# One transformer layer on one Trainium2 core: attention and last stage in one block with shared tiles, the first output projection between the last scores, the results added onto bias rows in memory

## What is computed

```python
x = x + attn(layernorm(x))      # 16 heads of 32; q = n @ Wq.T + bq + ocr_bias, k, v alike
                                # scores / sqrt(32) + 0.1 on |i - j| <= 2, softmax over 2048 keys, attn @ v
                                # out @ Wo.T + bo
x = x + ffn(layernorm(x))       # n and the weight are rounded per block of 32 to a 6-bit float grid times
                                # the block's scale (largest |n| / 7.5); then n_q @ w_q.T + bias
```

## Time and profile before

| | |
|---|---|
| median of 3 runs | 4273.5 us |
| the profiled execution | 4276.86 us |
| span of that execution, first to last instruction | 4275.0 us |
| mean granted TensorE clock | 0.983 |
| busy: TensorE, weight loads, VectorE, ScalarE, GpSimd | 97%, 60%, 77%, 56%, 70% |
| DMA queue of software (GpSimd's), share of 16 engines | 47.1% |
| DMA queue of hardware (SP's), share of 16 engines | 26.1% |

### The profile page before, as it was taken

The page is one execution under the profiler, slowest core; times in us unless marked ns, Lnnn a source line. Parts: engine busy times, 40 slices in busy tenths (PEclk is TensorE's granted clock), DMA queues, the critical chain, the costliest instruction groups (busy, mean ns, idle before and its releaser), DMA issues. The chain is left out here.

```text
span 4275.0 us, 60956 instructions
## 1 busy us (share of the span) xinstructions
PE 4150.8 (97%) x21904; PEld 2568.5 (60%) x21904; DVE 3302.9 (77%) x5623; ACT 2406.3 (56%) x4652; POOL 2988.7 (70%) x1047
## 2 busy tenths in 40 slices
PE   7999989999999999999999999999999999959999
PEld 6888855555555555555555555555555555527777
DVE  6444449888888888888888888888888888727776
ACT  2222215666667666666766666666666666633222
POOL 2111115888888888888888888888888888846552
PEclk9999988999999999999999999999999999979999
DMA  7666665888878878787887878878888787675442
GB/s 257 205 208 207 206 180 106 165 182 168 182 164 173 183 168 187 156 186 162 188 172 170 176 167 187 169 172 169 183 167 188 158 176 166 138 177 179 160 160 73
DMA packets 274636, 741.24 MB, mean 173 GB/s; under 512 B 27585, under 2 KB 94145, under 8 KB 220098
## 3 DMA queue, kind: packets, MB, share of 16 engines
q0 software_dynamic: 55296, 402.68, 47.1%
q1 hardware_dynamic: 219074, 335.10, 26.1%
HBM read 195.04 MB, written 139.46 MB: 78 GB/s over the span
## 5 line engine op out<-in xcount | busy, mean ns | idle before, releaser
L725 DVE TENSOR_REDUCE part_max<-ps_m 128x1 f32<-128x512 f32 x4096 | 2512.1, 679 | 441.9 <-PE ps_m L624 441.8
L790 POOL TENSOR_TENSOR pair<-p_sb 128x2048 f32<-128x2048 f32 x512 | 2419.4, 4769 | 259.8 <-ACT p_sb L715 148.8
L715 ACT ACTIVATE p_sb<-ps_s 128x512 f32<-128x512 f32 x4096 | 2083.3, 616 | 748.7 <-PE ps_s L643 745.3
L643 PE MATMUL ps_s<-q_st,k_st 97*128 97x512 f32 x4096 | 1685.9, 412 | 3.8 <-ACT p_sb L715 1.9
L624 PE MATMUL ps_m<-k_st,q_st 96*128 96x512 f32 x4096 | 1641.7, 404 | 20.3 <-POOL k_st L779 20.1
L643 PEld LDWEIGHTS ps_s<-q_st,k_st 97*128 97x128 f32 x4096 | 772.1, 189 | 648.3 <-issue 422.5
L657 PE MATMUL ps_o<-p_sb,v_sb 128*32 128x512 f32 x8192 | 988.0, 599 | 15.0 <-DVE p_sb L752 6.9
L624 PEld LDWEIGHTS ps_m<-k_st,q_st 96*128 96x128 f32 x4096 | 786.7, 192 | 191.5 <-DVE part_max L725 37.8
L657 PEld LDWEIGHTS ps_o<-p_sb,v_sb 128*32 128x32 f32 x8192 | 224.3, 109 | 493.1 <-ACT p_sb L715 310.3
L795 POOL DMA_DIRECT2D pair<-pair x384 | 336.2, 876 | 218.0 <-POOL pair L790 180.0
L172 POOL TENSOR_TENSOR xb<-xin,bo_row 128x2048 f32<-128x2048 f32 x16 | 75.3, 4703 | 428.6 <-DMA xin<-in_x 417.6
(11 more groups left out here) (97 smaller groups left out, 2621.6 us busy)
## 6 DMA issues: line engine op xcount, KB each, us to landing
pair<-pair POOLq DMA_DIRECT2D x384, 1024.0 KB, 8.6
q_st<-q_hi_d SPq DMA_DIRECT2D x128, 256.0 KB, 6.9
k_st<-k_hi_d SPq DMA_DIRECT2D x128, 256.0 KB, 9.3
xin<-in_x SPq DMA_DIRECT2D x16, 1024.0 KB, 8.3
xb_d<-xb SPq DMA_DIRECT2D x16, 1024.0 KB, 5.2
q_hi_d<-s_hi SPq DMA_DIRECT2D x64, 256.0 KB, 2.0
q_lo_d<-s_lo SPq DMA_DIRECT2D x64, 256.0 KB, 2.3
k_hi_d<-s_hi SPq DMA_DIRECT2D x64, 256.0 KB, 2.3
```

The lines of the kernel that those rows point to most:

```text
L643: nc.tensor.matmul(ps_s[:, (HG * s + h) % RING_S, :], k_st[0:ROWS + 1, unit // QC % 2, kt // TT, h, kt % TT * P:(kt % TT + 1) * P], q_st[0 ...
L715: nc.scalar.activation(p_sb[:, s % SLOTS, h, :], ps_s[:, (HG * s + h) % RING_S, :], ACT.Exp, scale=SCALE).then_inc(p_ready, 1)
L725: nc.vector.tensor_reduce(part_max[:, unit % 2, col, n:n + 1], ps_m[:, max_place(unit, j) % RING_M, :], AX.X, ALU.max).then_inc(max_taken, 1)
L790: nc.gpsimd.tensor_tensor(pair[:, m % PAIR_RING], p_sb[:, s % SLOTS], p_sb[:, (s + 1) % SLOTS], ALU.add).then_inc(paired, 1)
```

## The change

`attend` and `finish` become one function with one block. What it does:

- The barrier between the two stages goes. The last stage's tiles are laid over attention's: weights and `t_hi`, `t_lo`, `o_hi`, `o_rec` in `k_st`, `o_lo` in `q_st`, x1, `y`, `xd` and one `o_raw` in slots of `p_sb`, results in two slots of `pair`. `PAIR_RING` is 5. x1 and `xb` are one tile now (the residual is added in place), in a ring of 3; `o_rec` has one buffer in place of two.
- Chunk 0's output projection stands between the scores of the last unit, three matmuls behind every second score in steps 5 to 12. Chunks 0 and 1 are scaled and split on VectorE and ScalarE in that unit.
- The bias matmul of `linear` goes. In its place SP writes bias rows to the output in each of the first 16 units of attention, and the store of a chunk is an accumulating DMA issued by GpSimd.
- In the last stage, ScalarE's order is `high(c)`, `o_highs(c + 2)`, `normalise(c + 1)`; SP's is `load_o(c + 2)`, `load_rec(c + 2)`, `load_xb(c + 3)`.
- The sums of the last unit are finished inside the last stage.

```diff
-    PAIR_RING = 6
+    PAIR_RING = 5
+    FIRST_OUT = 5
...
+        o_first = sb("o_first", [P, NHG, CH])
+        o_hi, o_lo, o_rec = (k_st[:, 0, 0], q_st[:, 1]), (q_st[:, 0], q_st[:, 2]), f32(k_st[:, 0, 1])
+        wo_hi, wo_lo, wd_hi, wd_lo = k_st[:, 0, 2], k_st[:, 0, 3], k_st[:, 1, 0], k_st[:, 1, 1]
+        t_hi, t_lo = k_st[:, 1, 2], k_st[:, 1, 3]
+        x1 = (p_sb[:, 4], p_sb[:, 5], p_sb[:, 0])
+        y, xd, y_q = p_sb[:, 1], p_sb[:, 2], v_sb[:, 0:TT, :].bitcast(FP8)
+        res = (pair[:, 3], pair[:, 4])
+
+        def o_raw(c):
+            return p_sb[:, 3] if c > 1 and c % 2 == 0 else o_first
...
+            def load_o(c):
+                at_least(sp, o_split, NHG * (1 if c == 1 else c - 1))
+                sp.dma_start(o_raw(c)[:], o_by_chunk[c]).then_inc(o_in[c % 2], 16)
+
+            def load_rec(c):
+                at_least(sp, o_scaled, NHG * c)
+                sp.wait_ge(rec_out, 16 * (NG - QC + c // QC + 1))
+                for g in range(NHG):
+                    sp.dma_start(o_rec[:, g, :],
+                                 rec_d[g * NCH + c].unsqueeze(1).to_broadcast([HG, HD, CH])).then_inc(rec_in, 16)
+
+            def load_xb(c):
+                at_least(sp, res_ready, TT * (c - 2))
+                sp.dma_start(x1[c % 3], xb_d[c]).then_inc(xb_in[c % 3], 16)
...
+                    if unit < NCH and kt == 13:
+                        sp.dma_start(out_ch[unit], ffn_b.unsqueeze(0).unsqueeze(0).to_broadcast([P, TT, D])).then_inc(bias_out, 16)
...
+                    if unit == NU - 1 and kt == KT - 1:
+                        sp.wait_ge(pv_done, ST - 4)
+                        sp.wait_ge(paired, NM - 2)
+                        load_xb(0)
+            load_xb(1)
+            sp.wait_ge(scored, HG * ST)
+            sp.dma_start(f32(wd_hi), wd_hi_d).then_inc(wd_in, 16)
+            sp.dma_start(f32(wd_lo), wd_lo_d).then_inc(wd_in, 16)
+            sp.wait_ge(pv_done, ST)
+            sp.wait_ge(paired, NM)
+            load_xb(2)
+            for c in range(NCH):
+                if c + 2 < NCH:
+                    load_o(c + 2)
+                    load_rec(c + 2)
+                if c + 3 < NCH:
+                    load_xb(c + 3)
+                if c == 1:
+                    store_sum(NU - 1)
+                    load_den(NG - 1)
+                if c == 3:
+                    store_rec(NG - 1)
...
+            def between_scores(kt, h):
+
+                t, k = (kt - FIRST_OUT) // 2, (kt - FIRST_OUT) % 2 * 2 + h // 2
+                if h % 2 == 0 or not 0 <= t < TT:
+                    return
+                if k == 0:
+                    pe.wait_ge(max_taken, turn_no(NU - 1) + 1)
+                    if t == sum_place(NU - 2) % RING_M:
+                        pe.wait_ge(sum_copied, NU - 1)
+                out_part(0, t, k)
...
+            for c in range(NCH):
+                high(c)
+                if c + 2 < NCH:
+                    o_highs(c + 2)
+                if c + 1 < NCH:
+                    normalise(c + 1)
...
+            def store(c):
+                pool.wait_ge(res_ready, TT * c + TT)
+                pool.dma_start(out_ch[c], res[c % 2], accum_op=ALU.add).then_inc(out_done[c % 2], 16)
...
-                    nc.tensor.matmul(ps_r[:, t, :], ones2[:], fb[:], start=True, stop=False)
```

More of the change, by code:

```diff
@@ L569, in _ @@
                     if unit > 0:
-                        if kt == 8:
+                        if kt == 8 and unit < NU:
                             store_sum(unit - 1)
@@ L665, in add_keys @@
                     for h in range(HG):
-                        last = nc.tensor.matmul(ps_m[h * HD:(h + 1) * HD, bank, :], ones[:],
+                        last = nc.tensor.matmul(sum_bank(unit)[h * HD:(h + 1) * HD, :], ones[:],
                                                 pair[:, (PAIRS * unit + n) % PAIR_RING, h, :],
@@ L676, in burst, with out_part @@
                     add_keys(s // KT - 1)
+            def out_part(c, t, k):
+                if t == 0:
+                    pe.wait_ge(o_split, NHG * c + k + 1)
+                toks = slice(t * P, (t + 1) * P)
+                terms = ((o_hi[c % 2][:, k, toks], wo_hi[:, k, :]), (o_lo[c % 2][:, k, toks], wo_hi[:, k, :]),
+                         (o_hi[c % 2][:, k, toks], wo_lo[:, k, :]))
+                for j, (lhs, rhs) in enumerate(terms):
+                    if c == 0 and t == 0 and k == 0 and j != 1:
+                        pe.wait_ge(wo_in[j // 2], 16)
+                    last = nc.tensor.matmul(ps_r[:, t, :], lhs, rhs, start=(k == 0 and j == 0),
+                                            stop=(k == NHG - 1 and j == 2))
+                if k == NHG - 1:
+                    last.then_inc(out_projected, 1)
@@ new lines, in scale_o, with o_low @@
+            def scale_o(c):
+                v.wait_ge(o_in[c], 16)
+                v.wait_ge(rec_in, 16 * NHG * (c + 1))
+                for g in range(NHG):
+                    nc.vector.tensor_tensor(o_raw(c)[:, g, :], o_raw(c)[:, g, :], o_rec[:, g, :],
+                                            ALU.mult).then_inc(o_scaled, 1)
+            def o_low(c):
+                for g in range(NHG):
+                    v.wait_ge(o_high, NHG * c + g + 1)
+                    nc.vector.tensor_tensor(o_lo[c][:, g, :], o_raw(c)[:, g, :], f32(o_hi[c][:, g, :]),
+                                            ALU.subtract).then_inc(o_split, 1)
@@ L1088 @@
+                if c > 2:
+                    store(c - 3)
+            for c in range(NCH - 3, NCH):
+                store(c)
 def kernel(L0_attn_x, L0_attn_ocr_context, L0_attn_Wq, L0_attn_bq, L0_attn_Wk, L0_attn_bk, L0_attn_Wv,
```

477 lines of the change are left out of this document (210 added, 267 removed).

## The result

| | before | after |
|---|---|---|
| median of 4 runs | 4274.93 us | 4426.3 us (4424.11 to 4430.55) |
| ratio, 95% interval | | 1.0354 (1.0339 to 1.037) |
| span of the profiled execution | 4275.0 us | 4423.6 us |
| mean granted TensorE clock | 0.983 | 0.963 |

The kernel got 3.5% slower: 151 us more, where the prediction had 86. The sign and the loop are as forecast, and the time is 18 us above the upper end of the range. One execution of the last experiment was slow (4392.93 us at a granted clock of 0.893, its other five 4239.84 to 4247.28); its median of 4244.77 us counts it and is 4243.87 without.

What follows compares the result with a forecast made beforehand. TensorE bounded the last stage before; after the change a 37 us loop through the loads would: 3834 + 13 x 37 = 4315, then 23 and 22.7 more, span 4361, median 4359 us. Range 4320 to 4408.

Steps and rivals of the forecast that it cites:

- the loop: Last stage, one chunk's results to the next's through loads, scaling and normalisation: 37 us a chunk, bounds 34.0 and 43.
- the last unit: Attention's final unit: added matmuls and two `o_highs` show as +8 us, bounds 4 and 15.
- R(0): Moment VectorE finishes the last tile of chunk 0's results: 3834, 59 us earlier than before, 8 us either side.
- The 2 tenths: DMA engines' busy share while 1 MB of reciprocals loads: four of 16 engines, about 100 GB/s, 10.2 us.
- attention unchanged up to the last unit: Listed as a sign to see in the trace after: attention before its final unit keeps its length.
- The start of the last stage: From VectorE free near 3791 to chunk 0's results at 3834, with 4 MB of loads from 3789 on.
- The bias matmul is the other 0.43: In each tile of `linear`: 3.38 us step less 2.95 of products leaves 0.43, so 1.7 us saved per chunk.
- The bias rows: 16 MB written during attention, ahead of the next `put_shift`: 0 to 1 us a unit, 16 times at most.
- The tail: Chunk 14's results to end of span: 20.35 less 1.7 plus about 4 for the accumulating store, 22.7 us.
- The loads in time: Rival: last stage's loads come in time, TensorE stays the bound at 24.4 us a chunk, 4197 us; 4 in 100.
- The shorter loop of 30 to 33 us: Rival: in the last stage reciprocals move beside the other loads, 30.6 us a chunk, level with before; 7 in 100.
- The rival with a longer loop: Rival: accumulating stores or attention's costs, 41 us and up a chunk; at 42, 4424 us; 12 in 100.

Runs made afterwards that it cites:

- the last experiment: Fastest kernel (load edits plus chunk 2's reciprocals early) with bias rows issued right behind the shift row, not ahead of it: 4244.77 us, 0.9928.
- the first experiment: Changed kernel with loads of output weights, chunk 0's o and its reciprocals moved from step 12 to step 15 of unit 60: 4398.03 us.
- the bias edit alone: Kernel before the change, with bias rows written in attention, no bias matmul and accumulating stores by GpSimd: 4262.07 us, 0.997.
- three small edits: Changed kernel with shift row ahead of the loads, loads one chunk ahead and reciprocals over 16 engines: 4212.26 us, 0.9847.

## Why the prediction was right, and where it was wrong

| step of the prediction | predicted | measured in the change |
|---|---|---|
| attention up to unit 62 | unchanged | +38.1 us |
| the last unit | +8 | +19.3 (65.7 against 46.4) |
| from there to R(0) | 40.4 | 53.9 |
| R(0) | 3834 | 3896.9 |
| the loop, c = 1 to 13 | 37 | 36.8 |
| R(13) to R(14) | 23 | 22.2 |
| R(14) to the end | 22.7 | 26.7 |
| end of span | 4361 | 4423.6 |

R(0) to R(13) is 3896.9 to 4374.8; the end is 62.6 us late, and R(0) alone is 62.9 late.

**The loop was right.** "R(c - 1) and R(c) are tied by a closed loop, whatever TensorE does", of 18.8 + 5.7 + 12.3. In the trace: 19.1 from R to the scaling, 5.6 to the last rounding, 12.0 to R. The 2 tenths and the 10.2 us of reciprocals are there again, and the experiments with loads ahead and with 16 engines remove one and the other. The Trainium skill's rule (DMA: Bandwidth & Descriptors, "Why a DMA increments its semaphore by 16 and not by 1"), that a DMA uses no more engines than divide its slowest dimension, agrees with both.

**The step that failed is R(0) = 3834**, and in it "attention unchanged up to the last unit", which I had listed as a thing to see and never worked out. I followed SP's order in the new last stage, and did not follow what the change puts into SP's order in attention. The block of the first experiment's diff is part of the change: seven transfers in step 12 of unit 60, with the shift row behind them. Of the 38.1 us, moving that block alone gives back 28; the bias rows are about 12 over 16 units, of which 9 come back without them; and attention's first unit ended 4 us earlier (716.27 against 720.28), which is within the scatter, as that moment lies between 716 and 722 us in the traces of all the kernels. The prediction knew that 1 MB of reciprocals takes 10.2 us at four engines, but counted it only where their data are waited for. That issuing them holds SP, 35.60 us there, and that a small transfer stands behind them, is in none of its terms.

**The last unit** was mis-sized for that reason too: the matmuls and the two `o_highs` cost what I gave them (+8.8 us with 16 engines, with 8 predicted), and the other 10.5 are the load of o for chunk 1 behind the reciprocals; they are gone when only the shape of the reciprocals is altered. **The start of the last stage** (+13.5) is mis-sized in its loads. I had 4 MB issued from 3789 on, 4.6 us ahead of the last unit's copy. In the trace all but one `xb` stand behind the store of that unit's result and start at 3843.96, 1.0 us behind the copy; the reciprocals then land 35.3 us later, where I had some 25, and GpSimd waits 31.68 us for them. The four engines are only a small part of it, though they hold SP for 17.75 us: with 16 engines the start still takes 49.7 and 51.6 us, and 47.2 with the reciprocals of chunk 2 loaded early. What sets the rest isn't shown; two weights, two `xb` and o, 5 MB, go ahead of the reciprocals.

**The bias terms.** "The bias matmul is the other 0.43" is a duration read where a difference of starts was wanted. Without it, twelve products take 10.88 / 4 = 2.72 us, not 2.95, and so it is 3.38 - 2.72 = 0.66 us per tile, 2.6 per full chunk, where the prediction had 1.7; over the 14 chunks from R(0) to R(14) the bias edit alone gave 32 us. This did not show in the change, since TensorE waits there. The bias rows, which I put at 16 us at most, cost about 12; the ring of 5 nothing, in the kernel before. The tail was 4 us longer than predicted. The last store landed in 8.9 us, close to the 8.7 taken, but the plain one that it replaces had landed in 4.2 us and not in the median of 5.2, and from the landing to the end of the span it is 2.8 us where it had been 0.5. What these 2.8 us are isn't shown.

**The rivals.** The loads in time needed a different order in SP's program; with it, TensorE is the bound, as that rival said. The shorter loop of 30 to 33 us did not come: the 2 tenths begin again only when the full slices end. The rival with a longer loop gave 4424 us, and 4426.3 was measured; but it had the time right for a reason that isn't there, since the loop is 36.8 us and not 42. Of its two conditions only the bias rows' part in attention came true, 12 of its 65 us. That it hit is luck. A forecast that hits by a wrong mechanism would have led to the wrong repair.

What remains open: why SP's issue is held so much longer at one place (35.60 us) than at another (6.86 in the loop) for the same four transfers; 20 us later, in the first experiment, it was 20.27. More lay ahead of them there, with the pair transfers beside them, but this wasn't taken apart.

## What to carry to other kernels

When a change lays one stage's first loads into the stage before, write out the whole program of the issuing engine there, and for each small transfer that another engine waits for, sum what is issued ahead of it. A load may stand behind a wait for a result only if its data are not needed on the way to the next result; moving it one place turned 4426 into 4267 us. And before an edit is judged by its sum, look at it with the bound that it removes: here the same change is worth 1.5% with three small edits in the order and shape of its loads.

## What the runs showed of the hardware

- Issuing four transfers of 256 KB that use four DMA engines kept SP for 35.60, 17.75, 6.86 and 4.23 us at four places of one kernel. Spread over 16 engines the same bytes took 1.7 to 4.0 us in the last stage and in unit 60, though 12.1 and 12.5 at one place of the start.
- A transfer of one row, issued on time behind 4 MB on the same queue, landed after 28.5 us; issued ahead of them it took 4.3.
- Reads of 1 MB that fetch each row 32 times went at 200 to 260 GB/s with the 16 engines full, where loads beside them reached 400.
- An accumulating store of 1 MB to memory landed in 8.9 us (8.6 to 9.7) with the loop, and in 13.9 (8.8 to 15.5) in the kernel with the bias edit alone; a plain one had taken 5.2.
- A matmul with 2 rows took 0.66 us out of a tile, half as much again as its own 0.43 in the chain.
